# Cross-attention stage of a Perceiver block: the query and key weights multiplied on chip into one projection

## The reference, cut to what matters

```
q = layernorm(x) @ Wq + bq
k = ctx @ Wk + bk
v = ctx @ Wv + bv
attn = softmax(q @ k.T / sqrt(256))
x = x + attn @ v
```

## Time and profile before

| | us |
|---|---|
| median of 3 runs | 693.16 |
| lowest and highest | 692.3, 693.25 |
| span of the profiled execution | 691.0 |
| TensorE busy in the span | 652.4 |
| VectorE busy | 478.0 |
| ScalarE busy | 366.9 |

### The profile page before, as it was taken

One profiled execution on the slowest core, in us unless ns is written; L12 is line 12 of the kernel. 1 busy time (PEld: TensorE's weight loads), 2 busy tenths in 40 slices (PEclk: granted clock), 3 DMA queues, 4 the chain that ended last, 5 costly groups with the idle time before them and its releaser, 6 DMA issues. The chain is left out here.

```text
span 691.0 us, 11279 instructions
## 1 busy us (share of the span) xinstructions
PE 652.4 (94%) x4226; PEld 453.9 (66%) x4226; DVE 478.0 (69%) x820; ACT 366.9 (53%) x675; POOL 223.3 (32%) x180
## 2 busy tenths in 40 slices
PE   3999999998997998999999999999999999999997
PEld 2455555564335555666656688887777777888897
DVE  5123343357858999999999755678987778777554
ACT  2311111125559889899998832434466556455342
POOL 2000000000005999999897200024563020222000
PEclk9999999999999999999999999999999999999999
DMA  8999999965530223222221000000100012120000
GB/s 311 392 349 420 417 421 419 384 210 167 138 95 30 92 101 111 95 104 111 92 92 61 1 1 0 17 0 9 43 2 3 1 62 77 47 62 1 32 0 31
DMA packets 31070, 86.45 MB, mean 125 GB/s; under 512 B 7901, under 2 KB 19577, under 8 KB 28841
## 3 DMA queue, kind: packets, MB, share of 16 engines
q1 hardware_dynamic: 30456, 85.28, 33.8%
q10 hardware_dynamic: 560, 0.46, 0.3%
HBM read 83.50 MB, written 1.11 MB: 122 GB/s over the span
## 5 line engine op out<-in xcount | busy, mean ns | idle before, releaser
L702 POOL TENSOR_TENSOR dbu<-du,bs 128x1024 f32<-128x1024 f32 x63 | 148.8, 2387 | 215.3 <-DVE du L910 206.4
L1040 PE MATMUL Y<-weighed,ident 128*128 128x512 f32 (+1 forms) x256 | 100.0, 513 | 0.0
L932 DVE TENSOR_TENSOR_SCAN w_in<-hS,dbu 128x1024 f32<-128x1024 f32 x42 | 95.1, 2275 | 0.0
L794 ACT ACTIVATE weighed<-T,CT 128x256 f32<-128x256 f32 x208 | 82.8, 476 | 12.3 <-PE T L1029 10.7
L783 ACT ACTIVATE hS<-delta,negA 128x504 f32<-128x504 f32 x128 | 83.4, 695 | 4.5 <-DVE xn L932 3.6
L1040 PEld LDWEIGHTS Y<-weighed,ident 128*128 128x128 f32 x256 | 43.7, 190 | 30.6 <-issue 30.6
L932 DVE TENSOR_TENSOR_SCAN xn<-hS,dbu 128x1024 f32<-128x1024 f32 x22 | 50.1, 2279 | 4.2 <-issue 3.1
L1029 PE MATMUL T<-ident,w_in 128*128 128x128 f32 x336 | 45.1, 276 | 7.5 <-ACT weighed L794 3.5
L1029 PEld LDWEIGHTS T<-ident,w_in 128*128 128x128 f32 x336 | 36.5, 140 | 23.2 <-DVE w_in L932 20.7
L270 PE MATMUL O<-cN,pT 128*64 128x256 f32 x384 | 46.7, 385 | 0.0
L258 PE MATMUL S<-cT,qkT 128*64 128x512 f32 (+1 forms) x256 | 46.3, 514 | 0.0
(11 more groups left out here) (421 smaller groups left out, 1354.0 us busy)
## 6 DMA issues: line engine op xcount, KB each, us to landing
cT<-in_ctxT SPq DMA_DIRECT2D x8, 3202.0 KB, 17.5
cN<-in_ctx SPq DMA_DIRECT2D x8, 3072.0 KB, 16.9
bs<-b_rows SPq DMA_DIRECT2D x32, 512.0 KB, 3.6
raw_w<-in_w SPq DMA_DIRECT2D x16, 256.0 KB, 2.8
w<-in_w SPq DMA_DIRECT2D x7, 256.0 KB, 8.4
vs<-vx SPq DMA_DIRECT2D x8, 136.0 KB, 2.3
x<-in_x SPq DMA_DIRECT2D x2, 512.0 KB, 5.9
cR<-in_ctx SPq DMA_DIRECT2D x1, 1024.0 KB, 31.8
```

The source lines that it names most:

```text
L702: e.tensor_tensor(dbu[s % NB][:, :, :], half(m.du, s // DS), row, ALU.mult).then_inc(s_bu, 1)
L794: i = e.activation(weighed[s % 2][:, q * Q:(q + 1) * Q], T[:, q * Q:(q + 1) * Q], ACT.Copy, scale=c_of(s, q))
L932: e.tensor_tensor_scan(S[s % NS], A[s % 2][:, :], dbu[s % NB][:, :, :].rearrange("p c n -> p (c n)"), 0.0, ALU.mult, ALU.add).then_inc(s_h, 1)
L1040: e.matmul(Y[:, w], k.ident[:, :], weighed[s % 2][:, w], start=opens, stop=True, skip_group_check=True).then_inc(s_y, 1)
```

## The change: what it does

Wq and Wk.T are first multiplied on chip into one 256 x 256 matrix (`fold`), and then each half of the tokens is projected once, straight into `qkT`. For this TensorE transposes wq0 (4 transposes), VectorE copies the result to `wqT` with bq as an extra column, TensorE multiplies `wqT` with wk0T (4 matmuls of 256 columns), and ScalarE copies the product over wq0 (`keep_fold`). bq becomes a column `qcol` (4 one-column matmuls) that ScalarE adds while it moves the projection. The number q @ bk of each query is now made by VectorE (`key_bias`): TensorE spreads the row bk @ Wq.T over all partitions of `X` (2 matmuls of 257 columns), and VectorE multiplies the normalised tokens, which lie in `prob`, by that row (128 x 1024 for each half), sums over the width, adds a constant and scales. The loads change their order: the second half of x comes behind the weights.

```diff
@@ cross_attention @@
-        qT = k.xn[:, :, :].rearrange("p t d -> p (t d)").rearrange("p (c n) -> p c n", c=KD)
+        spare = k.xn[:, :, :].rearrange("p t d -> p (t d)")
+        wqT = spare[:, 0:KD * (D + 1)].rearrange("p (c n) -> p c n", c=KD)
+        qcol = spare[:, 3 * D:3 * D + KD]
+        qconst = spare[:, 3 * D + KD:3 * D + KD + 1]
+        qraw = spare[:, 4 * D:4 * D + TILES]
+        wqk = k.wq0
...
@@ tensor @@
-        pblocks = [(part, m, h) for h in range(2) for part in range(2) for m in range(KD)]
+        pblocks = [(m, h) for h in range(2) for m in range(KD)]
+            def fold():
+
+                for c in range(KD):
+                    for r in range(KD):
+                        i = e.transpose(O[:, c * D + r * P:c * D + (r + 1) * P], k.wq0[:, r, c * P:(c + 1) * P], k.ident[:, :])
+                i.then_inc(s_fold, 1)
+                for m in range(KD):
+                    for c in range(KD):
+                        i = e.matmul(tps[1][:, m:m + 1], k.wk0T[:, c, m * P:(m + 1) * P], col(k, "bq0", c),
+                                     start=c == 0, stop=c == 1)
+                i.then_inc(s_fold, 1)
+                e.wait_ge(s_fv, 1)
+                for r in range(KD):
+                    for c in range(KD):
+                        i = e.matmul(tps[0][:, r * D:(r + 1) * D], wqT[:, c, r * P:(r + 1) * P], k.wk0T[:, c, :],
+                                     start=c == 0, stop=c == 1)
+                i.then_inc(s_fold, 1)
+                for c in range(KD):
+                    i = e.matmul(X[:, 0:D + 1], col(k, "bk0", c).to_broadcast([P, P]), wqT[:, c, :], start=c == 0, stop=c == 1)
+                i.then_inc(s_fold, 1)
+
             def project(half):
                 e.wait_ge(s_e0, 2 * half + 2)
-                for n in range(4 * half, 4 * half + 4):
-                    part, m, h = pblocks[n]
-                    if n == 2:
+                if half == 0:
+                    e.wait_ge(s_fs, 2)
+                for n in (2 * half, 2 * half + 1):
+                    m, h = pblocks[n]
+                    if n == 1:
                         turn_first(1)
                     if n >= 2:
-                        e.wait_ge(s_pe, n if n % 4 == 2 else n - 1)
-                    w, src = ((k.wq0, k.xT), (k.wk0T, qT))[part]
+                        e.wait_ge(s_pe, n - 1)
                     for c in range(KD):
-                        i = e.matmul(tps[n % 2][:, :], w[:, c, m * P:(m + 1) * P],
-                                     src[:, c, h * HALF:(h + 1) * HALF], start=c == 0, stop=c == 1)
+                        i = e.matmul(tps[n % 2][:, :], wqk[:, c, m * P:(m + 1) * P],
+                                     k.xT[:, c, h * HALF:(h + 1) * HALF], start=c == 0, stop=c == 1)
                     i.then_inc(s_pp, 1)
-                if half:
-                    e.wait_ge(s_q0, 1)
-                for t in range(4 * half, 4 * half + 4):
-                    for c in range(KD):
-                        i = e.matmul(X[:, t:t + 1], qT[:, c, t * P:(t + 1) * P], col(k, "bk0", c),
-                                     start=c == 0, stop=c == 1)
-                i.then_inc(s_qb, 1)
...
             turn_first(0)
             e.wait_ge(k.s_w0, k.n_w0)
+            fold()
             project(0)
-            e.wait_ge(s_pe, 4)
+            e.wait_ge(s_pe, 2)
             scores(0)
             project(1)
             e.wait_ge(s_q0, 2)
-            e.wait_ge(s_pe, 8)
+            e.wait_ge(s_pe, 4)
             for i in range(1, TILES + 2):
                 if i <= TILES:
                     e.wait_ge(s_ex, i)
@@ scalar @@
-            def move(first, end):
-                for n in range(first, end):
-                    part, m, h = pblocks[n]
-                    e.wait_ge(s_pp, n + 1)
-                    if n == 6:
-                        e.wait_ge(s_pe, 6)
-                    if part == 0:
-                        e.activation(qT[:, m, h * HALF:(h + 1) * HALF], tps[n % 2][:, :], ACT.Identity,
-                                     bias=col(k, "bq0", m)).then_inc(s_pe, 1)
-                    else:
-                        e.activation(qkT[:, m, h * HALF:(h + 1) * HALF], tps[n % 2][:, :], ACT.Copy
-                                     ).then_inc(s_pe, 1)
+            def keep_fold():
+                e.wait_ge(s_fold, 2)
+                e.activation(qcol, tps[1][:, 0:KD], ACT.Copy).then_inc(s_fs, 1)
+                e.wait_ge(s_fold, 3)
+                e.activation(wqk[:, :, :], tps[0][:, :].rearrange("p (c n) -> p c n", c=KD), ACT.Copy).then_inc(s_fs, 1)
+
+            def move(n):
+                m, h = pblocks[n]
+                e.wait_ge(s_pp, n + 1)
+                e.wait_ge(s_fs, 1)
+                e.activation(qkT[:, m, h * HALF:(h + 1) * HALF], tps[n % 2][:, :], ACT.Identity, bias=qcol[:, m:m + 1]
+                             ).then_inc(s_pe, 1)
 
             def softmax(i):
                 if i >= 2:
@@ -387,15 +411,16 @@
             root_first(0)
             move_first(0)
             move_first(1)
+            keep_fold()
             root_first(1)
-            e.wait_ge(k.s_w0, k.n_w0)
-            move(0, 4)
+            move(0)
             move_first(2)
             move_first(3)
+            move(1)
             e.activation(warm[:, :], k.ident[:, 0:1], ACT.Exp)
-            move(4, 5)
+            move(2)
             softmax(0)
-            move(6, 8)
+            move(3)
             for i in range(1, TILES + 2):
                 if i >= 2:
                     e.wait_ge(s_ot, i - 1)
@@ vector @@
+                if half == 0:
+                    e.wait_ge(k.s_w0, k.n_w0)
+                    e.tensor_copy(wqT[:, :, D], k.cols[:, COLS["bq0"][0]:COLS["bq0"][0] + KD])
+                    e.wait_ge(s_fold, 1)
+                    e.tensor_copy(wqT[:, :, 0:D], O[:, :].rearrange("p (c n) -> p c n", c=KD)).then_inc(s_fv, 1)
...
-            def scale_qbk(half):
+            def key_bias(half):
                 at = slice(4 * half, 4 * half + 4)
-                e.wait_ge(s_qb, half + 1)
-                e.tensor_scalar(qbk[:, at], X[:, at], scale, None, ALU.mult).then_inc(s_q0, 1)
+                xs = prob[half][:, 0:4 * D].rearrange("p (t d) -> p t d", d=D)
+                if half == 0:
+                    e.wait_ge(s_fold, 4)
+                    e.tensor_copy(qconst, X[:, D:D + 1]).then_inc(s_qr, 1)
+                e.wait_ge(s_t0, 2 * half + 2)
+                e.tensor_tensor(xs, xs, X[:, 0:D].unsqueeze(1).to_broadcast([P, 4, D]), ALU.mult).then_inc(s_qr, 1)
+                e.wait_ge(s_qr, 2 * half + 2)
+                e.reduce_sum(qraw[:, at], xs, AX.X).then_inc(s_qr, 1)
+                e.wait_ge(s_qr, 2 * half + 3)
+                e.tensor_scalar(qbk[:, at], qraw[:, at], qconst, scale, ALU.add, ALU.mult).then_inc(s_q0, 1)
 
...
-            scale_qbk(0)
+            key_bias(0)
+            key_bias(1)
             maximum(0)
-            e.wait_ge(s_pp, 6)
-            e.wait_ge(s_pe, 5)
-            e.tensor_scalar(qT[:, 1, HALF:TOK], tps[1][:, :], col(k, "bq0", 1), None, ALU.add).then_inc(s_pe, 1)
-            scale_qbk(1)
             for i in range(1, TILES + 2):
                 if i <= TILES:
                     for g in range(2):
@@ sync, first loads @@
-                for half in range(2):
-                    ts = slice(4 * half, 4 * half + 4)
-                    e.dma_start(k.x[:, ts, :], tiles[:, ts, :]).then_inc(k.s_x[half], 16)
+                e.dma_start(k.x[:, 0:4, :], tiles[:, 0:4, :]).then_inc(k.s_x[0], 16)
                 for n, w in (("wq0", k.wq0), ("wk0T", k.wk0T)):
                     e.dma_start(w[:, :, :], t[n].rearrange("(c p) n -> p c n", p=P)).then_inc(k.s_w0, 16)
+                e.dma_start(k.x[:, 4:8, :], tiles[:, 4:8, :]).then_inc(k.s_x[1], 16)
```

More of the change, by code:

```diff
@@ L145, in cross_attention @@
         s_pe = sem("a_pe")
-        s_qb = sem("a_qb")
+        s_fold = sem("a_fold")
+        s_fv = sem("a_fold_dve")
+        s_fs = sem("a_fold_act")
+        s_qr = sem("a_qr")
         s_q0 = sem("a_q0")
```

## The result

The changed kernel takes 696.41 us, median of 15 runs (694.57 at the lowest), the kernel before 693.3 beside it (692.3 at the lowest). The ratio is 1.0037, with a 95% interval of 1.0025 to 1.0048: slower. The ratio is estimated from the fast runs alone (14 of each 15; one of each was slow), so it is not the quotient of the two medians, which is 1.0045. The profiled execution has a span of 693.1 us and took 694.9, so it is one of the cheaper ones. 695.0 was forecast.

A forecast was written before the change was run, and what follows sets the result against it. The prediction took the landing of cT of tile 2 to gate scores(2), with TensorE bounding the tiles from there. Span 691.0 - 0.1 + 2.0 = 692.9, with 2.16 on top 695.1, stated as 695.0 us; range 692.8 to 696.5.

The forecast's parts named there:

- The gate: At scores(2): cT of tile 2 still lands at 56.83, so the gain kept is 0.2 us at most.
- Rival C: Ahead of scores(2): cT of tile 2 lands earlier after all, 6.6 us are kept, 686.5 us; chance 0.06.
- The first part: Ahead of scores(2): scores(0) starts at 20.1 to 21.8 instead of 24.68, scores(1) at 32.5 to 33.5 instead of 41.79.
- The wait: Straight before scores(2): TensorE stands 3 to 6.4 us for cT of tile 2.
- The price of the wait: At scores(2): TensorE begins at the low clock and loses 2.0 us, between 1.44 and 2.55.
- Rival B: At scores(2): the wait eats the gain but the clock stays up or soon rises again, 693.0 us; chance 0.25.
- VectorE: Beside scores(0): key_bias takes 2.8 us a half, ends at 25.9, and delays maximum(0) by no more than 0.5.
- Behind the gate: After the wait at scores(2): nothing else changes, a tile takes 15.04 us as before.
- The sum: Whole span: 691.0 - 0.1 + 2.0 = 692.9 us, with 2.16 on top 695.1, stated as 695.0.
- its own case: Whole kernel: the forecast of 695.0 us, with a range of 694.3 to 695.9; chance 0.60.
- the 2.16 on top of the span: Whole kernel: the profiled execution before lay 2.16 us below the median of the runs, added at the end.
- D: Up to scores(2): TensorE arrives after 57, or the low clock lasts through all of scores(2), 698.7 us; chance 0.09.

The follow-up runs named there:

- e5: The changed kernel with sixteen idle TensorE matmuls of 256 columns put into the wait ahead of scores(2): 692.98 us, ratio 0.9994 to the kernel before.
- e2: The changed kernel with ten idle TensorE matmuls of 256 columns put into the wait ahead of scores(2): 694.24 us, ratio 1.0008 to the kernel before.
- e4: The changed kernel with SyncE issuing cT of tile 2 before cN of tile 1: 687.4 us, ratio 0.9904 to the kernel before.
- e8: e4 with the first loads in the old order, both halves of x and then the weights: 687.84 us, ratio 0.9911 to the kernel before.
- e1: The changed kernel run again with no edit: 696.49 us, ratio 1.0032 to the kernel before.
- e6: The kernel before with eight idle TensorE matmuls of 128 columns ahead of turn_first(0): 697.13 us, ratio 1.0032 to the kernel before.
- e10: e4 with cR loaded in two parts, batches 0 to 3 ahead of cT of tile 2, the rest behind cN of tile 1: 689.84 us.
- e11: e4 with eight idle TensorE matmuls at the start, those of e6: 689.75 us, ratio 0.9939 to the kernel before.
- e9: e4 without key_bias's multiplications and sums on VectorE: 688.08 us, ratio 0.9909 to the kernel before.

## Why the prediction was right, step by step

- **The gate.** Forecast: cT of tile 2 lands at 56.83 whatever the first part does. It landed at 57.48 and 57.35 in the two traces of the changed kernel, at 57.3 in e5 and at 56.84 in e2. e4 shows that it is the bytes ahead of it that set it: 6.6 us earlier as soon as the 3.15 MB of cN of tile 1 go behind (by 420 GB/s they would take 7.5, an estimate). Rival C (the landing moves by itself when scores(0) is early) is out, since scores(0) was 3.2 us early and the issue still came at 30.78 behind a blocked one.
- **The first part.** scores(0) was forecast at 20.1 to 21.8 and came at 21.45; scores(1) at 32.5 to 33.5, came at 33.12. This agreement is partly luck. I read the x8 behind 3.70 us as eight matmuls, where the code issues four (each stands there twice). The fold's four matmuls at the low clock take 3.76 us (e5, e8), not 1.7; in the first trace the clock was already high for them (1.97). In the other traces (e1, e2, e4, e5) scores(0) starts at 23.8 to 24.3 and scores(1) at 35.5 to 35.9, 2 us or more outside both forecasts. There the fold takes back nearly all that it saves ahead of scores(0) (24.68 before), and the gain comes between scores(0) and scores(1). The mistake cost nothing, since the wait for cT covers it: e1, 2.4 us later at scores(0), is even 3.0 us earlier at scores(2) (49.6), because cR had landed at 41.0 and no fall of the clock lay between.
- **The wait.** 3 to 6.4 us were forecast; 4.9 and 7.8 were measured. 7.8 lies outside: the forecast let values(0) start no earlier than 41.95, and e1 has it at 41.07 and needs 8.5 us from there.
- **The price of the wait.** Forecast 2.0, between 1.44 and 2.55; measured 1.51 and 2.52. The Trainium skill's rule in "TensorE: Matmul & The Clock Gate" ("HAM oscillation — how this bites in real kernels") says that a wait for a transfer between bursts of matmuls drops the clock and the next burst starts cold. It holds here in each of the five traces with a wait of 2.6 us or more ahead of scores (changed, e1, e2, e6, e10) and behind the two long waits ahead of values(0) (changed, e11); in none of them does the clock stay up. Not every burst starts cold, though: in e6 and at values(0) of the changed kernel the clock is still high when the work begins and falls 0.9 us into it (at 59.95 and 43.5). e4 and e5, with 0.2 and 0.4 ahead of scores(2), show no fall there. Rival B is out in these traces.
- **VectorE.** Forecast 2.8 a half, measured 1.21 + 1.22 + 0.23; done at 25.5, before scores(0) ends at 27.05. e9 confirms that it costs nothing.
- **Behind the gate.** Forecast no change; 15.05 us a tile in both kernels, and 558.8 and 558.7 from scores(7) to the end.
- **The sum.** Forecast +1.9 for the span (-0.1 + 2.0), measured +2.1 in the profiled execution. That closeness is partly luck too: the later landing added 0.45, where 0.1 was to be saved, and the clock cost 1.51 of the 2.0. The time was 1.4 above the forecast: 696.41 lies 0.5 above the range that the prediction gave its own case (694.3 to 695.9) and only 0.1 below the upper end of the whole range. The term that came out too small is the 2.16 on top of the span, taken from the kernel before: here the median lies 3.3 above it. The medians differ by 3.1 (the ratio gives 2.6, interval 1.7 to 3.3). The part of it beyond 2.1 fits e1's larger price and the late fall of the clock, but how often each occurs in either kernel can't be told from one trace per kernel, and stays open. Open too is why cT of tile 2 landed at 57.3 to 57.5 in three traces after the change, and at 56.83 before and 56.84 in e2; one trace of the kernel before can't tell a shift from chance, and e6 has it at 59.06. One slip in the chances: D has 0.09 and is added into "slower" as 0.08.

## What to carry to other kernels

Before work is taken out ahead of a double-buffered stage, add up when each transfer lands and who waits for it: a saving counts only up to the first landing that it can't move, and past that point nothing more is gained, while a fall of TensorE's clock costs time on top (here 1.4 to 2.8 us behind waits of 2.6 to 7.8). Make the saving and the move of the gating transfer as one change (here -3.1 us became +5.8), and if the transfer can't move, idle matmuls that fill the whole wait can keep the clock up (e5); filling it in part left the fall in e2's trace.

## What the runs showed of the hardware

- The profile's granted clock reads 1.00 from the start (1.00 over 12 to 17 in the kernel before), while the spacing of matmuls shows half speed until about 17.6 in the kernel before; so here a row of the clock is no evidence ahead of its first fall.
- While the 1 MB of cR is moved, in rows of 1 KB to 65 partitions, the transfers are slow: in e4 141, 205 and 175 GB/s in three windows of 2.5 us from 32.5 to 40, with the DMA engines full, against 420 elsewhere:

```profile
32.50:35.00 2.50, 1.24 (x7) 0.72 (x6) 0.00 (x0) 1.71 (x3) 0.00 (x0) 1.00 0.96 141
35.00:37.50 2.50, 2.50 (x15) 1.14 (x15) 1.29 (x2) 0.00 (x0) 0.00 (x0) 1.00 1.14 205
37.50:40.00 2.50, 2.50 (x14) 0.86 (x12) 0.00 (x0) 0.00 (x0) 0.00 (x0) 1.00 1.08 175
```

- That it is cR is shown by e10, which moves three quarters of it later: a second slow stretch comes with them, between 50 and 59 (the lines are its first three us). Whether the short rows or the few partitions make it slow isn't separated.

```profile
50.00:51.00 1.00, 1.00 (x8) 0.37 (x6) 0.25 (x1) 0.07 (x1) 0.00 (x0) 1.00 1.09 221
51.00:52.00 1.00, 1.00 (x8) 0.34 (x6) 0.00 (x0) 0.00 (x0) 0.00 (x0) 1.00 0.95 145
52.00:53.00 1.00, 1.00 (x6) 0.28 (x4) 0.00 (x0) 0.00 (x0) 0.00 (x0) 1.00 1.11 194
```

- The price of a wait doesn't follow its length: 1.42 us lost behind 2.8 (e2), 1.70 behind 3.7 (e6), 1.51 behind 4.9 (changed), 2.52 behind 7.8 (e1), but 2.84 behind 2.6 (e10). What counts is how much of the low stretch falls on work. In the first trace of the changed kernel the clock fell only as the work came (1.51 lost), in e1 5 us sooner, and stayed low until about 62.5, 5.2 us into the work (2.52 lost). In e10 it fell at about 66 and was low for the first 5.7 us of the work. Why it stays low for different lengths isn't shown.
